# Attention value products of two steps issued together, in one run of sixteen matmuls

## The reference

```python
xn = layernorm(x)
q, k, v = split(xn @ w_attn + b_attn)          # 16 heads of 8
scores = q k^T / sqrt(8) + mask                # mask: -log(distance + 1) for later keys, -inf for earlier ones
attention = (softmax(scores) v) @ w_proj + b_proj
ffn = fp4_linear(silu(fp4_linear(xn, w_gate)) * fp4_linear(xn, w_up), w_down)
out = x + attention + ffn
```

## Time and profile before

| | us |
|---|---|
| time, median of 3 runs | 627.31 (627.09 to 627.82) |
| time of the profiled execution | 626.35 |
| its span, first to last instruction | 624.5 |
| outside the span | 1.85 |
| PE busy | 564.4 (90% of the span) |
| DVE busy | 562.8 (90%) |
| POOL busy | 537.4 (86%) |
| ACT busy | 400.8 (64%) |

### The profile page before, as it was taken

One profiled execution on the slowest core, in us unless ns is written; L12 is line 12 of the kernel. 1 busy time (PEld: TensorE's weight loads), 2 busy tenths in 40 slices (PEclk: granted clock), 3 DMA queues, 4 the chain that ended last, 5 costly groups with the idle time before them and its releaser, 6 DMA issues.

```text
span 624.5 us, 11270 instructions
## 1 busy us (share of the span) xinstructions
PE 564.4 (90%) x3807; PEld 250.9 (40%) x3807; DVE 562.8 (90%) x1178; ACT 400.8 (64%) x857; POOL 537.4 (86%) x400
## 2 busy tenths in 40 slices
PE   6999779999999999999989899999989898989985
PEld 5576534444343334333333332342334242432322
DVE  6899998989999999999999999998989999997661
ACT  4576457566656475767667577666656667759782
POOL 7226987789899989999998999999998999998992
PEclk9999988999999999999999999999999999999997
DMA  5255341310000000200000000000000000000000
GB/s 148 74 137 114 119 83 51 78 43 36 2 2 3 0 2 10 86 1 2 2 0 2 19 1 1 2 2 1 1 2 1 19 0 2 1 2 1 1 2 17
DMA packets 14715, 16.66 MB, mean 27 GB/s; under 512 B 1594, under 2 KB 14171, under 8 KB 14243
## 3 DMA queue, kind: packets, MB, share of 16 engines
q1 hardware_dynamic: 14123, 15.70, 9.2%
q10 hardware_dynamic: 536, 0.26, 0.2%
HBM read 11.75 MB, written 4.01 MB: 25 GB/s over the span
## 4 chain that ended last, share of the span: by engine, by line
PE 43%; POOL 32%; DVE 13%; ACT 7%; issue 4%; ACTq 0%; POOLq 0%; DVEq 0%
POOL ring L802 25%; PE psum L1396 11%; PE psum L1354 9%; PE psum L1378 7%; DVE mxp L1135 7%; ACT ring L954 2%; POOL xw L820 2%; POOL xw L818 2%; PE psum L1331 2%; POOL xw L822 2%; PE psum L1312 2%; PE psum L1314 1%; PE psum L1320 1%; DVE ring L1162 1%; PE psum L1404 1%
## 5 line engine op out<-in xcount | busy, mean ns | idle before, releaser
L802 POOL TENSOR_TENSOR ring<-ring,dist 128x1024 f32<-128x1024 f32 (+3 forms) x223 | 438.4, 1996 | 31.7 <-ACT ring L954 31.3
L1135 DVE TENSOR_REDUCE mxp<-psum 128x1 f32<-128x512 f32 (+3 forms) x640 | 352.6, 598 | 20.5 <-PE psum L1354 11.4
L954 ACT ACTIVATE ring<-psum 128x512 f32<-128x512 f32 (+3 forms) x446 | 211.5, 528 | 101.5 <-PE psum L1381 51.9
L1354 PE MATMUL psum<-kop,qop 96*128 96x512 bf16 (+3 forms) x640 | 198.0, 352 | 7.3 <-DVE mxp L1135 5.3
L1378 PE MATMUL psum<-qop,kop 128*128 128x512 bf16 (+3 forms) x640 | 190.7, 349 | 6.2 <-DVE mxp L1135 3.7
L1396 PE MATMUL psum<-ring,vaug 128*32 128x512 f32 (+3 forms) x1280 | 151.5, 544 | 15.0 <-POOL ring L802 14.1
L1162 DVE TENSOR_TENSOR ring<-psum,dist 128x512 f32<-128x512 f32 (+3 forms) x194 | 115.7, 622 | 13.9 <-ACT psum L954 13.8
L954 ACT ACTIVATE psum<-psum 128x512 f32<-128x512 f32 (+3 forms) x194 | 99.5, 543 | 39.7 <-PE psum L1378 23.4
L1354 PEld LDWEIGHTS psum<-kop,qop 96*128 96x128 bf16 x640 | 57.2, 97 | 127.8 <-DVE mxp L1135 46.5
L1378 PEld LDWEIGHTS psum<-qop,kop 128*128 128x128 bf16 x640 | 59.7, 97 | 82.2 <-DVE mxp L1135 15.5
L1357 PE MATMUL psum<-tri_q,identb 128*128 128x128 bf16 x256 | 56.2, 221 | 0.0
(11 more groups left out here) (130 smaller groups left out, 490.2 us busy)
## 6 DMA issues: line engine op xcount, KB each, us to landing
kop<-parts_dram SPq DMA_DIRECT2D x9, 384.0 KB
qop<-parts_dram SPq DMA_DIRECT2D x9, 384.0 KB
parts_dram<-qpart SPq DMA_DIRECT2D x18, 128.0 KB, 2.8
xin<-_attn_hidden_states_dram SPq DMA_DIRECT2D x4, 256.0 KB, 4.7
ring<-inv_dram SPq DMA_DIRECT2D x1, 1024.0 KB, 4.9
out_dram<-xin SPq DMA_DIRECT2D x4, 256.0 KB, 2.3
parts_dram<-qpart SPq DMA_DIRECT2D x6, 96.0 KB
qop<-parts_dram SPq DMA_DIRECT2D x3, 192.0 KB
```

Of the source, the lines that this page charges most:

```text
L802: g_.tensor_tensor(slot(p)[:, :, 0:n], slot(p)[:, :, 0:n], both, ALU.mult).then_inc(weighed_pool, 1)
L954: a_.activation(scores if pair_vec[p] else slot(p)[:, e % 2, 0:n], scores, ACT.Exp, scale=SCALE).then_inc(exp_done, 1)
L1135: v_.tensor_reduce(mxp[:, u % 2, 4 * a + j, c - g:c - g + 1], bank(*o)[:, 0:n], AX_X, ALU.max).then_inc(max_used, 1)
L1354: ins = mm(bank(*o)[:, 0:n], qop[0:K_MAX, u // NQ % 2, h, P * a:P * (a + 1)], kop[0:K_MAX, h, k0:k0 + n], start=True, stop=(c != g))
```

## The change

Steps 2k and 2k+1 are treated as a pair. The plan takes the value product of an even step only when the needs of the odd step behind it are met as well, and then gives the odd one rank 0, ahead of everything else on PE. The plan's price for a switch is charged to the even step alone. No instruction is added or removed; their order on PE changes, and with it what the plan gives to all engines.

```diff
-        pe(("pv", s), 4 * P * blocks[s] + PV_SWITCH, needs, rank=5)
+        pe(("pv", s), 4 * P * blocks[s] + (0 if s % 2 else PV_SWITCH), needs, rank=5)
...
         if engine == "PE":
             free = len(free_banks(now))
-            if kind in ("pv", "hT", "down", "warm"):
+            if kind == "pv":
+                if item[1] % 2:
+                    return 0
+                second = ready(engine, queues["PE"]["pv"][item[1] + 1], now)
+                return level if second is not None and second <= now else None
+            if kind in ("hT", "down", "warm"):
                 return level
```

## The result

The kernel with pairs takes **648.07 us** (median of 4 runs, 645.75 to 649.77) against 627.2 before: a ratio of 1.033 (95%: 1.029 to 1.037), 20.9 us slower. The sign is the forecast's. The size isn't: 6.9 us were forecast, a third of it, and the time lies just beyond the end of the range (648). The profiled execution took 649.43 us, its span is 647.5.

A forecast was written before the change was run, and what follows sets the result against it. No single engine was taken as the bound: PE, DVE and POOL are all nearly full. 626.35 us profiled + 13.3 of waits - 6.4 saved = 633.3, plus 0.96 to the median: 634.2 us, range 619 to 648.

The forecast's parts named there:

- The saving: Value products on PE: 79 pairs each save 0.19 us of switches, 15.0 us of PE time, worth 6.4 us.
- rival 3: Joint between a pair's two steps isn't seamless: all eight weight loads stand between them; 643.3 us, chance 0.03.
- A run of 2.0 us in which PE feeds nobody: Behind paired value products DVE waits for maxima: 29.6 us of new waits, counted as 13.3 us of time.
- the twelve value products with gate and up behind them: In the old trace, runs of 2.28 us on PE; DVE waited 11.2 us over all twelve, 0.93 each.
- twelve gate and up products behind pairs: Gate and up behind a pair makes a 3.2 us run on PE: some 0.3 us more DVE wait for each of twelve.
- Rival 4: The ring of four steps fills because the held even step keeps its slots, holding ACT, then POOL; 648 us, chance 0.08.
- The test named in the prediction: ACT's waits for the value products (L1396, after: L1401) far over 1.9 us would show the ring filling.
- PE's 10.3 us of waiting may halve: PE's waits for POOL's weights before value products may halve, worth 0 to 2 us; taken as 0.
- The end stage: Last 54 us, maxima done: eight full pairs may cost ACT 0.5 us each, 0 to 4 us; taken as 0.
- The chain's shares: Prices from the chain of waits: PE's saving counts at 0.43, a DVE wait at 0.45 (DVE 0.13 plus POOL 0.32).

The follow-up runs named there:

- pe61: Kernel before, all lists kept; on PE's list alone the even step's value product moved down to the odd one's for 61 pairs: 625.43 us, 0.9999.
- unless_full: Changed kernel, but an even step isn't held once the ring is full, and the odd one has rank 0 only right behind an even one: 634.75 us.
- apart: Changed kernel, but the odd step keeps its old rank, so the even step is still held while runs stay short: 631.11 us, 1.0075.
- pe_up: Kernel before; on PE's list alone 19 other pairs joined just before the first score needing the even step's slots: 640.24 us, 1.0205.
- after_ring7: Changed kernel with one ring slot fewer (SLOTS = 7): 663.89 us, 1.0588 against the kernel before.
- before_ahead33: Kernel before with three scores allowed ahead of the exponential instead of two (EXP_AHEAD = 3): 620.37 us, 0.9889.

## Why the prediction was right in sign and wrong in mechanism and size

**The saving.** Right in size: 13.7 us of busy time on L1401 against 15.0, and rival 3 fell, since all four groups start 0.42 to 0.46 us apart. So a third and a fourth set of weights load beside running matmuls of the same rows. The Trainium skill, on its page "TensorE: Matmul & The Clock Gate" (section "Part 3: Packing small matmuls — row/col tiling"), says that loads overlap only where the row groups differ; the trace disagrees between steps as it did within one. The same section also lets loads into a background weight buffer go ahead, and which buffer these took no run here shows. Wrong in worth: the forecast took 6.4 us by PE's share of the chain, and pe61, which freed 20 us of PE, gained nothing by its median and 1.6 us at the higher clock.

**"A run of 2.0 us in which PE feeds nobody."** This step failed. It priced a run by the twelve value products with gate and up behind them, at 29.6 us of new waits on DVE. The change brought 10.7, and pe61's 61 runs brought 1.0. Ten of the twelve runs did run dry, but that a run is long isn't enough for it; what else those places have in common no run here took apart. In the kernel after, what POOL lacks behind the run at 412.02 is scores, not maxima. The sum also counted on twelve gate and up products behind pairs; in the new order four stand there. So the forecast's sign came by luck: the waits that it was built on came at a third of their size, and the loss came with others, which its sum had at nothing.

**Rival 4, the ring.** This is the mechanism that the experiments speak for, and it had a chance of 0.08, because ACT waited only 1.9 us for a slot. That row couldn't have shown it. The plan doesn't put a score on PE's list until it has taken the value product that frees its slots, so with a full ring the score isn't issued at all: ACT waits for L1383 and L1386, POOL for ACT, and nobody for L1401. After the change, with POOL starved for 23.6 us more, those who waited for L1401 from 110 to 560 us are the copies out alone:

```profile
  ACT osb L984: 2.0, 3
```

The test named in the prediction (ACT's waits far over 1.9 us) would have cleared the culprit. That rival 4's 648 us is the measured time is luck as well: 13.3 us of it are the DVE waits of the forecast. Nor is the count of even steps at a full ring (5 before, 26 after) a measure of the loss: it is 16 in pe61, which lost nothing, 23 in unless_full and 33 in apart. What costs is a score that is issued later because its slots are given back later, and pe_up shows that at 0.67 us a pair.

**What is shown, and what is argued.** On the old lists, long runs that put no score behind a step which it could have gone ahead of cost nothing (pe61), and nineteen that do cost 12.7 us (pe_up). That the change itself loses by the same is argued from it: its plan is made anew on every engine, the hold brings even steps to a full ring, and the run then keeps scores back for 2 us more; without the hold there, 13.3 us come back (unless_full, whose split of the weights differs too), and holding with short runs costs 4 us (apart). No run keeps the changed plan's other lists and undoes its runs. For the rest, 6 to 8 us, three things are candidates that weren't told apart: the plan's split of the weights, the clock (3.6 us for what the fillers took away, some 10 for all of it at that rate, both loose), and the hold itself.

**The other parts.** "PE's 10.3 us of waiting may halve" came truer than that (0.9 us) and was worth nothing. The end stage is unchanged, as taken. The chain's shares (0.45 of a DVE wait, 0.43 of PE's saving) were the wrong price for both: what counted nearly one for one, in the kernel after and in pe_up, was POOL's idle time before its weights. Where the split changed too, POOL's busy time on weights belongs to it: over all thirteen changed kernels, the two together move with the span to within 4 us (unless_full 12.0 for 11.3, after_ring7 37.4 for 37.7, before_ahead33 -5.2 for -5.9).

## What to carry to other kernels

Time freed on one engine need not be worth anything where others are as busy; test the price of a longer run by moving one engine's list and leaving every other as it was. A step that is held back keeps its buffers, and where the order is fixed ahead, as here, a full buffer need not show as a wait for the instruction that frees it: it showed as starvation further down. So look in the program's order for the items that want those buffers and now stand behind the held step, and in the trace for how much later they start; a count of how often the buffer is full didn't give the loss. One more item in hand ahead of the starving engine gave 1.1% here, by another split of the work, where the change to the feeding engine gave a loss.

## What the runs showed of the hardware

Between matmuls of the same 128 rows and four column groups of 32, four sets of weights followed each other 0.42 to 0.46 us apart, with the third and fourth loaded while matmuls ran; joining 79 pairs took 13.7 us off the busy time of the value products, 0.17 us a pair. The 2.85 us of waiting that end at 424.28 were followed by a stretch at a granted clock of 0.54, and fillers in such waits cut the time at 1.2 GHz from 42.3 to 33.5 us, without a change in the kernel's time.
